# Attention with pairs of tiles folded in groups of four instead of three, and ScalarE rounding the result's high part

## What is computed

```
energy = jnp.einsum('bhqd,bhkd->bhqk', q, k)
att = jax.nn.softmax(energy, axis=-1) / D ** 0.5
out = jnp.einsum('bhqk,bhkd->bhqd', att, v)
...
out = out @ Wp.T + bp
h1 = out + hidden
h2 = _sln(h1, w, ln_g, ln_b, Wg, bg, Wb, bb)
return h2 + h1
```

## Time and profile before

| | |
|---|---|
| median of 3 runs | 2972.89 us (2970.24 to 2973.2) |
| the profiled execution | 2969.37 us |
| its span, first to last instruction | 2967.6 us |
| TensorE (PE) busy | 2866.0 us, 97% |
| GpSimd (POOL) busy | 1801.1 us, 61% |
| VectorE (DVE) busy | 2008.0 us, 68% |
| ScalarE (ACT) busy | 1508.9 us, 51% |
| folds: DMAs on q0 | 28.1% of the 16 DMA engines' time |
| SP's DMAs on q1 | 25.9% |

### The profile page before, as it was taken

The page is one execution under the profiler, slowest core; times in us unless marked ns, Lnnn a source line. Parts: engine busy times, 40 slices in busy tenths (PEclk is TensorE's granted clock), DMA queues, the critical chain, the costliest instruction groups (busy, mean ns, idle before and its releaser), DMA issues.

```text
span 2967.6 us, 41315 instructions
## 1 busy us (share of the span) xinstructions
PE 2866.0 (97%) x15018; PEld 1920.1 (65%) x15018; DVE 2008.0 (68%) x3559; ACT 1508.9 (51%) x2756; POOL 1801.1 (61%) x797
## 2 busy tenths in 40 slices
PE   4899999999999998999999999999999999999997
PEld 2787788888888886755555555555555555555456
DVE  7873332222333555778888888888888888888639
ACT  3552233232333321246666666666666666666644
POOL 2676310111110333248989999999989898988954
PEclk8999999999999999999999999999999999999999
DMA  6543100000001566586669876687856788666668
GB/s 216 173 144 119 52 19 11 29 29 29 29 15 58 182 221 203 180 200 122 137 131 196 167 157 137 130 178 167 185 121 146 147 187 179 136 134 139 162 199 301
DMA packets 155050, 405.64 MB, mean 137 GB/s; under 512 B 12101, under 2 KB 30505, under 8 KB 134342
## 3 DMA queue, kind: packets, MB, share of 16 engines
q0 software_dynamic: 22608, 164.64, 28.1%
q1 hardware_dynamic: 132248, 238.41, 25.9%
HBM read 144.51 MB, written 92.31 MB: 80 GB/s over the span
## 4 chain that ended last, share of the span: by engine, by line
PE 54%; DVE 1%; ACT 0%; DMA 0%; issue 0%; DVEq 0%; SPq 0%; ACTq 0%
PE psum L1714 18%; PE psum L1726 16%; PE psum L1699 15%; PE psum L1754 3%; PE psum L37 1%; PE psum L39 1%; PE psum L38 1%; DVE part_max L1835 1%; DMA p_att_lo<-att_parts 0%; DVE p_h L2141 0%; ACT probs L1805 0%; DVE p_h L2135 0%; PE psum L1705 0%; DVE p_stats L2147 0%; DVE p_var L2158 0%
## 5 line engine op out<-in xcount | busy, mean ns | idle before, releaser
L1835 DVE TENSOR_REDUCE part_max<-psum 128x1 f32<-128x512 f32 x1984 | 1211.7, 679 | 162.3 <-PE psum L1699 157.0
L1805 ACT ACTIVATE probs<-psum 128x512 f32<-128x512 f32 x2048 | 1042.4, 613 | 473.3 <-PE psum L1714 471.6
L1949 POOL TENSOR_TENSOR pair<-probs 128x2048 f32<-128x2048 f32 x204 | 937.6, 4596 | 139.5 <-ACT probs L1805 135.9
L1714 PE MATMUL psum<-queries,keys 128*128 128x512 f32 x2048 | 837.3, 411 | 7.6 <-PEq L2345 3.1
L1699 PE MATMUL psum<-keys,queries 128*128 128x512 f32 x1984 | 787.7, 398 | 0.6
L1714 PEld LDWEIGHTS psum<-queries,keys 128*128 128x128 f32 x2048 | 383.0, 187 | 341.3 <-issue 213.4
L1726 PE MATMUL psum<-probs,values 128*32 128x512 f32 x4096 | 510.0, 598 | 0.0
L1077 DVE TENSOR_TENSOR h_lo<-w_stage,h_hi 128x512 fp32r<-128x512 f32 x128 | 100.5, 786 | 486.4 <-ACT h_hi L986 486.3
L1699 PEld LDWEIGHTS psum<-keys,queries 128*128 128x128 f32 x1984 | 373.3, 188 | 75.5 <-DVE part_max L1835 18.9
L979 ACT ACTIVATE w_stage<-psum,b_col 128x512 f32<-128x512 f32 x128 | 88.3, 690 | 483.2 <-PE psum L39 482.4
L1726 PEld LDWEIGHTS psum<-probs,values 128*32 128x32 f32 x4096 | 106.8, 109 | 239.2 <-issue 123.1
(11 more groups left out here) (342 smaller groups left out, 3835.9 us busy)
## 6 DMA issues: line engine op xcount, KB each, us to landing
pair<-pair POOLq DMA_DIRECT2D x94, 1024.0 KB, 8.3
raw_weight<-pair POOLq DMA_DIRECT2D x32, 1024.0 KB, 8.4
pair<-raw_weight POOLq DMA_DIRECT2D x31, 1024.0 KB, 8.6
queries<-q_parts SPq DMA_DIRECT2D x96, 256.0 KB, 9.5
keys<-k_parts SPq DMA_DIRECT2D x42, 512.0 KB, 13.1
s_x<-in_x_dram SPq DMA_DIRECT2D x8, 1024.0 KB, 7.6
s_y<-in_x_dram SPq DMA_DIRECT2D x8, 1024.0 KB, 5.4
y_rows<-s_y SPq DMA_DIRECT2D x8, 1024.0 KB, 4.8
```

What stands on the lines that cost most here:

```text
L1714: nc.tensor.matmul(psum[:, SC + unit % 3, :], keys[place(count)[0]][:, h, kt * P:(kt + 1) * P], queries[count % NQ][:, h, :], start=True, ...
L1805: act.activation(probs[tile % NPROB][:, h, :], psum[:, SC + unit % 3, :], ACT.Exp).then_inc(exp_ready, 1)
L1835: dve.tensor_reduce(part_max[:, h * TT + qt, kc:kc + 1], max_slot(), AX.X, ALU.max).then_inc(max_read, 1)
L1949: pool.tensor_tensor(pair[number % NPAIR][:, :, :], probs[2 * number % NPROB][:, :, :], probs[(2 * number + 1) % NPROB][:, :, :], ALU.add) ...
```

## The change

In every block but the last the pairs form two groups of four. The total comes 8 tiles after a group's last tile everywhere. A group's first fold is issued as before. The second is issued in the middle of the add of the group's fourth pair, which is cut in two halves of two heads; the third behind the add of the next group's first pair. VectorE turns the sums in tile 9 and inverts them in tile 11. The rounding of the high part moves from POOL to ScalarE, in tile 3, two blocks later; that of block 30 comes at the end.

```
-    AV_LAG, SUM_LAG, LAST_LAG = 3, 10, 8
+    AV_LAG, SUM_LAG = 3, 8
...
-              for group in (((0, 1, 2), (3, 4, 5), (6, 7)) if count < BLOCKS - 1 else ((0, 1), (2, 3), (4, 5), (6, 7)))]
+              for group in (((0, 1, 2, 3), (4, 5, 6, 7)) if count < BLOCKS - 1 else ((0, 1), (2, 3), (4, 5), (6, 7)))]
...
+        def split_high(count):
+
+            act.wait_ge(weighed, count + 1)
+            act.wait_ge(att_st, 32 * (count + 1))
+            act.activation(att_hi[:, :], att[:, :], ACT.Copy).then_inc(att_split, 1)
+
...
+                if count > 1 and kt == 3 and h == 1:
+                    split_high(count - 2)
...
+        split_high(BLOCKS - 2)
         copy_out(BLOCKS - 1)
+        split_high(BLOCKS - 1)
...
+            if count > 0 and kt == 9:
+                turn_sums(count - 1)
             if count > 0 and kt == 11:
-                turn_sums(count - 1)
-            if count > 0 and kt == 13:
                 invert(count - 1)
                 spread_inverse(count - 1)
...
         def split_result(count):
-            pool.wait_ge(weighed, count + 1)
-            pool.wait_ge(att_st, 32 * (count + 1))
-            pool.tensor_copy(att_hi[:, :], att[:, :]).then_inc(att_split, 1)
             pool.wait_ge(att_split, count + 1)
...
-            if p == 6 and count == BLOCKS - 1:
-                split_result(count - 1)
...
-            pool.tensor_tensor(pair[number % NPAIR][:, :, :], probs[2 * number % NPROB][:, :, :],
-                               probs[(2 * number + 1) % NPROB][:, :, :], ALU.add).then_inc(pair_ready, 1)
-            if number in FOLDS and number - 1 not in FOLDS:
+            target, even, odd = pair[number % NPAIR], probs[2 * number % NPROB], probs[(2 * number + 1) % NPROB]
+            nth = GROUPS[OF[number]].index(number)
+            if nth == 3:
+                pool.tensor_tensor(target[:, 0:HG // 2, :], even[:, 0:HG // 2, :], odd[:, 0:HG // 2, :], ALU.add).then_inc(half_made, 1)
+                fold(number - 1)
+                pool.wait_ge(half_made, OF[number] + 1)
+                pool.tensor_tensor(target[:, HG // 2:HG, :], even[:, HG // 2:HG, :], odd[:, HG // 2:HG, :], ALU.add).then_inc(pair_ready, 1)
+            else:
+                pool.tensor_tensor(target[:, :, :], even[:, :, :], odd[:, :, :], ALU.add).then_inc(pair_ready, 1)
+            if nth == 1 and number in FOLDS:
                 fold(number)
-            if number - 1 in FOLDS and number - 2 in FOLDS:
+            if nth == 0 and number > 0 and len(GROUPS[OF[number - 1]]) == 4:
                 fold(number - 1)
+        split_result(BLOCKS - 2)
         normalise(BLOCKS - 1)
         split_result(BLOCKS - 1)
```

More of the change, by code:

```diff
@@ L1549, in attention_stage @@
     inverted, spread = sem("den_inverted"), sem("inverse_spread")
-    weighed, att_split = sem("att_weighed"), sem("att_split")
+    weighed, att_split, half_made = sem("att_weighed"), sem("att_split"), sem("half_made")
     SC, MX, OUT = 0, 3, 7
@@ L1574, in fold_wait @@
         engine.wait_ge(folded[n % 2], 16 * (n // 2 + 1))
-    SUMMED_AT = {2 * group[-1] + 1 + (SUM_LAG if group[-1] < PAIRS * (BLOCKS - 1) else LAST_LAG): g for g, group in enumerate(GROUPS[:DIRECT])}
+    SUMMED_AT = {2 * group[-1] + 1 + SUM_LAG: g for g, group in enumerate(GROUPS[:DIRECT])}
     WP_AT = (BLOCKS - 1) * NKT + 3
```

## The result

The changed kernel takes 3024.7 us (median of 4 runs, 3019.79 to 3028.0) against 2973.05 us: 51.6 us more, a ratio of 1.017 with a 95% interval of 1.0158 to 1.0182. The profiled execution has a span of 3026.2 us, against 2967.6.

What follows compares the result with a forecast made beforehand. The prediction took TensorE as the bound, with POOL nearly full. Its terms, -25.8 + 36 + 6 + 0.5 = +16.7 us, gave 2986 us for a profiled run and 2990 us for the median, range 2946 to 3014.

Steps and rivals of the forecast that it cites:

- What is removed: Totals of blocks 0 to 30 on TensorE: 31 fewer, 30 of them on the path at 0.86 us, 25.8 us gain.
- The folds: DMAs adding one pair to the next: in undisturbed blocks they land before the totals, with margins 2.9 and 2.7 us.
- The blocks that change keys: Six blocks with key loads: late folds stall totals 5.0 us at the end and 1.0 us mid-block, 36 us loss.
- the last boundary: Into block 31: folds alternate with pieces of 4 MB of other transfers, costing 6 us, bounds 0 and 9.
- L: Time when the loads at a block's end begin, 3.7 us after tile 15's slot; L = T-2.9.
- The turn of the sums moves two tiles earlier ... nothing on the path: VectorE's earlier turn spares POOL 0.73 us of waiting for the inverse and costs nothing on the path.
- ScalarE's copy: One 0.61 us copy a block moved to ScalarE: no cost except some 0.5 us in the last block.
- The last rival: POOL becomes the bound in every block, period 48.5 to 49.5 us, total 3021 us; chance 0.10.
- The first rival: Folds and loads interleave on the DMA queues, so no total waits; 2947 us; chance 0.27.

Runs made afterwards that it cites:

- the first run above: Total 10 tiles behind a group's last tile (8 in the last block), turn and inverse in tiles 11 and 13, against the changed kernel: 2991.63 us, ratio 1.0059.

## Why the prediction was wrong

The direction and the places of the waits were right, and so was the mechanism behind them, except for what it left out; the time was outside the range, 11 us above its upper end. Of the 35 us between the sum (+16.7) and the result (+51.6), 17.0 are a term that was missing, some 7 to 10 the turn, put at nothing, and 9 the size of the waits. By its steps:

- *What is removed*, 30 x 0.86 us: right. The run without loads gives 28.6 us, and the plain period with the late turn is 47.95 us against the 47.97 forecast.
- *The folds*, plain blocks keep their margins: right. No total of a plain block waits, and the rival in which GpSimd becomes the bound in every block is out.
- *The blocks that change keys*: the cause is shown by the run without the loads, the size was somewhat low. 5.0 us at a boundary measured 6.0 (36.2 / 6), 1.0 us in the middle 1.5 (9.1 / 6), 6 us at the last boundary 5.8. Together 51.1 us where the sum had 42. At the boundary shown, L is 1999.88: fold 6 landed at L+19.3 and fold 7 at L+27.9; I had taken L+15 to L+17 and L+25 to L+27. The deadline (2021.1, L+21.3) and the order of the transfers were right. What was mis-sized is the load ahead of fold 6: I let it end at L+9, but the hardware queue kept the DMA engines until L+11.6 and moved 1.9 MB in that time, the keys and part of what stood behind them. The fold's 6 us of data and the 2 us to its landing were right.
- *"The turn of the sums moves two tiles earlier ... nothing on the path"*: this step failed. I looked at VectorE's total air (145.0 us of waiting for matmuls) and not at where the turn, the inverse, the spread, the end of the maxima and the negation would then stand, close together in a ring of four PSUM slots. The cost is 0.34 us a block, 10.2 us in 30 blocks by the periods, and 6.6 us by the run with the late turn; the search matmuls' loads wait 40.5 us for VectorE, 20.9 with the turn back.
- *A term that was missing*: the half clock behind each long wait. The sum charged a stall with its own length and nothing for the work behind it, without a reason. It cost 17.0 us by the trace, and filling the seven long waits with work gave 13.0 us back. This is the largest part of the miss.
- *ScalarE's copy*, no cost: right, by the run with the rounding on GpSimd.

The sum with the traces' terms: the plain period falls from 48.84 to 48.29 us, which is -16.5 us in 30 blocks (the removed totals and the turn together); waits of totals +51.1; half clock +17.0. That gives 51.6 us, as measured. That it fits to the decimal is chance: the profiled executions differ by 58.6 us, of which 4.9 us are there by the first total (1339.21 and 1344.12), most of them from the stages ahead of attention.

The last rival's time (3021) lies nearest to the measured one, but by luck: its mechanism, a wait in every block, is absent.

The first rival (the transfers interleave, no total waits) is ruled out by the trace: fold 6 moved nothing while the hardware queue had 104.8%. The round-robin at packet granularity that the Trainium skill describes ("DMA: Bandwidth & Descriptors", Queues, rings and completion order) does not show at this scale: with a load of 1.5 MB issued 4.6 us ahead, the fold moved nothing for 7 us and then had 90.3%, beside 18.0% for the hardware queue.

What stays open: which waits let the clock fall. Behind waits of totals of 1.99 and 2.36 us it fell in the changed kernel, behind 1.89 us it did not; in the run with the fill it fell behind 2.21 and 3.04 us and stayed up behind 2.58. So the length of the wait alone does not decide, and no run varied it by itself. Open too is whether cutting the loads or moving them is what helped in the spread runs.

## What to carry to other kernels

A chain of dependent DMAs has to be costed where other transfers are densest, not at its median landing (7.1 to 7.4 us here, against 14.7 for the fold that set a stall). Spreading the foreign load in pieces helped in part (3024.7 to 2991.9 us) and was not enough, since each link can meet a piece. A stall of the engine that sets the pace has to be charged with more than its length, if the granted clock falls behind it. If the wait between links stands in the queue of an engine that does other work, that work is held up too; a later deadline alone then moves the stall to another engine. Savings per block can be kept by using the cheaper form only in the blocks in which nothing else is loaded: here, with the total 10 tiles behind and the late turn, 24 of 31 blocks with groups of four gave -23.2 us, where all 31 gave +15.5 (the first run above) and, with the change as it was made, +51.6.

## What was not expected of the hardware

- A wait of 4.66 to 7.15 us on TensorE is followed by a granted clock at the lower level for part of the work behind it (0.50 until about 2030.5 behind the wait that ended at 2027.82), so that a total takes 1.94 us instead of 1.04. Waits of 1.99 and 2.36 us were followed by it too. Replacing the long waits by useless matmuls makes the kernel faster (3011.7 against 3024.7 us).
- A fold's landing can be 2 us behind its last data: data until about 2017.5, landed at 2019.2, with the hardware queue at 115.2% in between.
- A fold that stands behind a load does not share with it: issued at 2004.52, it moved nothing until about 2011.5, while the hardware queue had 100 to 105% (2004 to 2010 us).
- GpSimd's add in two halves cost little: 2.42 us for the first 1024 columns (121.0 us for 50 of them in the page) and 2.69 for the second, behind the fold's issue, against 4.72 for a whole add of 2048 in the same kernel.
